# Routing per chunk into fixed regions of rows, and expert outputs added to the output by accumulating DMAs

## The reference

```python
x = x + attention(layernorm(x), Wq, bq, Wk, bk, Wv, bv, Wo, bo)   # 32 heads of 16, 8 key/value heads
xf = layernorm(x).reshape(2048, 512)
gate_logits = xf @ gate_w.T                                        # 8 experts
top_vals, top_idx = top_k(gate_logits, 2)
w = softmax(top_vals)
y = einsum('td,eod->teo', xf, expert_w) + expert_b
out = x + sum over the token's two experts of w * y
```

## Time and profile before

| | us |
|---|---|
| three runs | 1798.77, 1800.97, 1801.69 (median 1800.97) |
| the profiled execution | 1808.37 |
| its span | 1806.6 |
| PE, DVE, ACT, POOL busy | 1662.1, 1411.3, 1258.0, 485.4 |

### The profile page before, as it was taken

The page is one execution under the profiler, slowest core; times in us unless marked ns, Lnnn a source line. Parts: engine busy times, 40 slices in busy tenths (PEclk is TensorE's granted clock), DMA queues, the critical chain, the costliest instruction groups (busy, mean ns, idle before and its releaser), DMA issues.

```text
span 1806.6 us, 38059 instructions
## 1 busy us (share of the span) xinstructions
PE 1662.1 (92%) x13766; PEld 799.8 (44%) x13767; DVE 1411.3 (78%) x1401; ACT 1258.0 (70%) x2349; POOL 485.4 (27%) x730
## 2 busy tenths in 40 slices
PE   5999999999999999999999999999999979569970
PEld 3533444444444444444444444444444446328860
DVE  3287899999999999999999999999999316451214
ACT  2324788888888888888888888888888953313320
POOL 3121033222232233222223222222223351150016
PEclk9997899999999999999999999999999999669995
DMA  6346312321241232223121211121121331144447
GB/s 195 87 117 138 47 43 45 60 73 40 52 86 40 40 60 63 46 52 81 44 54 41 58 30 30 34 52 29 29 52 34 128 105 54 41 174 151 163 136 253
DMA packets 74539, 138.14 MB, mean 76 GB/s; under 512 B 19321, under 2 KB 23433, under 8 KB 73649
## 3 DMA queue, kind: packets, MB, share of 16 engines
q1 hardware_dynamic: 46352, 80.25, 18.4%
q0 software_dynamic: 25616, 54.21, 10.9%
q10 hardware_dynamic: 2448, 1.84, 0.6%
HBM read 82.61 MB, written 52.17 MB: 75 GB/s over the span
## 4 chain that ended last, share of the span: by engine, by line
PE 88%; POOL 3%; issue 2%; DMA 2%; DVE 2%; ACT 1%; ACTq 1%; SPq 0%; POOLq 0%; DVEq 0%
PE bank L815 33%; PE bank L776 24%; PE bank L805 16%; PE bank L896 8%; PE bank L748 3%; POOL slots_x L444 1%; PE bank L958 1%; POOL ys L453 1%; POOL xs L453 1%; DVE max_kc L1068 1%; PE bank L763 1%; DMA x_all<-in_L_attn_x 1%; PE bank L908 1%; DMA q_st<-q_parts 0%; PE bank L738 0%
## 5 line engine op out<-in xcount | busy, mean ns | idle before, releaser
L1068 DVE TENSOR_REDUCE max_kc<-bank 128x1 f32<-128x1024 f32 x1024 | 1241.5, 1222 | 84.7 <-PE bank L776 65.0
L652 ACT ACTIVATE arena_p<-bank 128x512 f32<-128x512 f32 x2048 | 1109.4, 595 | 171.3 <-PE bank L805 141.2
L815 PE MATMUL bank<-arena_p,v_cur 128*32 128x256 f32 x8192 | 660.5, 395 | 5.6 <-issue 5.6
L776 PE MATMUL bank<-k_st,q_st 48*128 48x512 f32 x2048 | 514.2, 500 | 5.3 <-DMA q_st<-q_parts 3.9
L805 PE MATMUL bank<-q_st,k_st 50*128 50x512 f32 x2048 | 449.6, 411 | 0.3 <-ACT arena_p L652 0.3
L776 PEld LDWEIGHTS bank<-k_st,q_st 48*128 48x128 f32 x2048 | 192.2, 185 | 434.4 <-issue 382.4
L805 PEld LDWEIGHTS bank<-q_st,k_st 50*128 50x128 f32 x2048 | 298.5, 187 | 35.4 <-ACT arena_p L652 22.4
L815 PEld LDWEIGHTS bank<-arena_p,v_cur 128*32 128x32 f32 x8192 | 163.1, 108 | 296.2 <-issue 155.0
L379 POOL DMA_DIRECT2D sums<-o_acc x128 | 63.9, 506 | 330.8 <-ACT o_acc L632 328.0
L1185 DVE TENSOR_TENSOR x2T_lo<-bank,x2T_hi 128x512 fp32r<-128x512 f32 x39 | 27.0, 692 | 105.8 <-ACT x2T_hi L662 105.8
L748 PE MATMUL bank<-xT,arena_p 128*128 128x512 f32 x160 | 82.4, 639 | 2.8 <-ACT xT L592 2.8
(11 more groups left out here) (151 smaller groups left out, 913.3 us busy)
## 6 DMA issues: line engine op xcount, KB each, us to landing
q_st<-q_parts SPq DMA_DIRECT2D x192, 128.0 KB, 4.7
slots_x<-be_sb POOLq DMA_DIRECT2D x39, 256.0 KB, 2.4
xs<-slots_x SPq DMA_DIRECT2D x39, 256.0 KB, 2.7
slots_y<-ys SPq DMA_DIRECT2D x39, 256.0 KB, 2.0
q_parts<-parts SPq DMA_DIRECT2D x16, 512.0 KB, 3.0
we_raw<-in_L_ffn_expert_w POOLq DMA_DIRECT2D x8, 1024.0 KB, 6.1
at_parts<-o_hl POOLq DMA_DIRECT2D x128, 64.0 KB, 2.2
k_st<-k_parts SPq DMA_DIRECT2D x48, 128.0 KB, 4.7
```

Source lines behind the costliest of these rows:

```text
L652: act.activation(probs[:, u % PRING, :], bank[:, ring_bank(("score", u)), :], ACT.Exp, scale=SCALE).then_inc(p_ready, 1)
L776: return pe.matmul(bank[:, 2 + 2 * (m % 2) + q, :], q_st[r:r + CROW, j % SLOTS, h, qt * P:(qt + 1) * P], k_st[r:r + CROW, j // NC % KSLOTS ...
L815: mm = pe.matmul(bank[32 * h:32 * h + 32, 6, half], v_cur[:, kt, :], probs[:, (REP * kt + h) % PRING, half], start=(kt == 0 and part == 0) ...
L1068: dve.reduce_max(max_kc[:, m:m + 1], bank[:, 2 + 2 * (m % 2):4 + 2 * (m % 2), :].rearrange("p a s -> p (a s)"), AX.X).then_inc(m_done, 1)
```

## The change

The region of an expert is now fixed: expert e owns the rows from e x 2048 on, so that a chunk's tokens can be placed as soon as that chunk's logits are there. `slots_x` grows from 39 to 135 tiles of rows (8 x 16 and 7 spare ones), and a row from 512 to 516 values: behind the normalised token stand its number, its first expert and the difference of its two logits (twice). All 135 tiles are prefilled with a row whose token number, 4095, lies beyond the output; this takes one DMA of 5 tiles per round, in 27 rounds, and stands between `divide_outputs` and `shift_lo`.

Choosing, ranking and placing run once per chunk of 4 tiles, between tiles of the output projection. After chunk 1, 2048 pairs are placed, and at least S1 = 9 tiles of them are full; these are listed (`full_tiles`) and go through the expert pass first. The other 30 are listed in four parts between the first tiles of the expert pass (`other_tiles`), after the last chunk's rows are known.

The normalised tile is made by ACT in place (`normalise_tile`), after SP has stored the residual tile to the output (`store_residual`). POOL, not DVE, subtracts five of the eight expert matrices. In the expert pass DVE works out each row's gate from the values behind the row (`row_gates`), ACT multiplies by it, DVE adds the gated bias (`row_bias`), and POOL adds the tile to the output rows with an indirect accumulating DMA (`add_rows`), each issued only when the one before has landed. `slots_y`, the biases' matmuls and the gathering are gone.

```diff
@@ POOL
+            def fill_rows(z):
+                n = min(FILL, NX - z)
+                if z > 0:
+                    pool.wait_ge(fill_dma, 16 * (z // FILL))
+                pool.dma_start(slots_x[z * P:(z + n) * P, :].rearrange("(n p) d -> p n d", p=P),
+                               pad_row[:, :].unsqueeze(1).to_broadcast([P, n, W])).then_inc(fill_dma, 16)
...
                 divide_outputs(i)
+                if FILL * (i - 1) < NX:
+                    fill_rows(FILL * (i - 1))
                 if i < N - 1:
                     shift_lo(i + 1)
...
-            for n in range(NKT):
-                pool.wait_ge(xn2_ready, n + 1)
+            def scatter(n):
+                pool.wait_ge(xg_ready, n + 1)
                 for a in range(2):
                     pool.indirect_dma_start(slots_x, bass.IndirectOffsetOnAxis(ap=slot_i[:, a, n:n + 1], axis=0),
-                                            xn2[:, n % SR, :], None).then_inc(sc_dma[n % SR], 16)
+                                            x2_all[:, n, :], None).then_inc(sc_dma[n // TT], 16)
+            def add_rows(s):
+                pool.wait_ge(yb_ready, s + 1)
+                if s > 0:
+                    pool.wait_ge(add_dma, 16 * s)
+                pool.indirect_dma_start(out_rows, bass.IndirectOffsetOnAxis(ap=tok_i[:, s % TRING, :], axis=0),
+                                        ys[:, s % SR, :], None, bounds_check=T - 1, oob_is_err=False,
+                                        compute_op=ALU.add).then_inc(add_dma, 16)
...
+            for e in range(POOL_LO):
+                expert_lo(e)
+            for c in range(NC - 1):
+                pool.wait_ge(slots_ready, c + 1)
+                for t in range(TT):
+                    scatter(c * TT + t)
+            pool.wait_ge(slots_ready, NC)
+            for t in range(TT):
+                add_rows(t)
+                scatter((NC - 1) * TT + t)
+            for s in range(TT, NS):
+                add_rows(s)
@@ SP
+            for c in range(EARLY_C):
+                sp.wait_ge(sc_dma[c], 32 * TT)
+            sp.wait_ge(list_ready, 1)
+            for s in range(SR):
+                load_slots(s)
+            sp.dma_start(x2_all[:, 0:E, 0:D], expert_b.partition_broadcast(P)).then_inc(be_dma, 16)
+            for s in range(SR, S1):
+                load_slots(s)
+            for c in range(EARLY_C, NC):
+                sp.wait_ge(sc_dma[c], 32 * TT)
+            sp.wait_ge(list_ready, 2)
@@ ACT
+            def output_evac(s):
+                n, b = number(s), ring(s)
+                act.wait_ge(y_full, n + 1)
+                act.wait_ge(gate_ready, n + 1)
+                if not first_pass(s):
+                    act.wait_ge(add_dma, n * 16 - 16 * (SR - 1))
+                act.activation(ys[:, b, :], bank[:, b, :], ACT.Identity, scale=gate[:, b, :]).then_inc(y_evac, 1)
@@ PE
             def logits_back(k):
                 pe.wait_ge(lgT_ready, k + 1)
+                if k > 0:
+                    pe.wait_ge(rank_read, k)
@@ DVE
+            for n in range(NKT):
+                residual_add(n)
                 if n == 1:
                     reciprocal_sums(N)
+                statistics(n)
+                scaling(n)
+                if n >= 7 and n % TT == 3:
+                    choose_experts(n // TT - 1)
+                if n >= 9 and n % TT == 1:
+                    place_rows(n // TT - 2)
+                if n == TT * EARLY_C + 6:
+                    full_tiles()
+                if n >= 14:
+                    expert_lo(n - 9)
+            expert_lo(E - 1)
...
+            def row_bias(s):
+                n, b = number(s), ring(s)
+                expert = dve.value_load(expert_i[0:1, bass.ds(n, 1)], min_val=0, max_val=E - 1)
+                dve.wait_ge(y_evac, n + SR + 1)
+                dve.scalar_tensor_tensor(ys[:, b, :], x2_all[:, bass.ds(expert, 1), 0:D].squeeze(1), gate[:, b, :],
+                                         ys[:, b, :], ALU.mult, ALU.add).then_inc(yb_ready, 1)
...
+            place_rows(NC - 2)
+            choose_experts(NC - 1)
+            dve.wait_ge(list_ready, 1)
+            transposed_lo(0)
+            row_gates(0)
+            for s in range(HEAD):
+                slot_step(s)
+                if s == 1:
+                    place_rows(NC - 1)
+                if 2 <= s < 6:
+                    other_tiles(s - 2)
```

More of the change, by code:

```diff
@@ L305, in preln_attention_moe, with number, lap, later @@
         B_MAX = ring_bank(("maxima", 0))
+        HEAD, UNROLL = S1 + 1, TRING
+        LAPS = (NS - HEAD) // UNROLL
+        REST = HEAD + LAPS * UNROLL
+        def number(s):
+            return s if isinstance(s, int) else HEAD + s[0] * UNROLL + s[1]
+        def lap(s):
+            return s // SR if isinstance(s, int) else s[0] * (UNROLL // SR) + (HEAD + s[1]) // SR
+        def later(s, d):
+            return s + d if isinstance(s, int) else (s[0], s[1] + d)
+        def ring(s, size=SR):
+            return (s if isinstance(s, int) else HEAD + s[1]) % size
+        def first_pass(s):
+            return isinstance(s, int) and s < SR
         block = ctx.enter_context(nc.Block())
@@ L571, in _ @@
+            for s in range(SR, S1):
[3 more added lines that the diff above has]
+            sp.wait_ge(list_ready, 2)
+            for s in range(S1, HEAD):
+                load_slots(s)
+            with sp.Fori(0, LAPS) as m:
+                for j in range(UNROLL):
+                    load_slots((m, j))
+            for s in range(REST, NS):
+                load_slots(s)
         @block.scalar
@@ new lines, in slot_step @@
+            def slot_step(s):
+                if s != NS - 1:
+                    transposed_hi(later(s, 1))
+                    difference_exp(later(s, 1))
+                output_evac(s)
+            transposed_hi(0)
+            difference_exp(0)
+            for s in range(HEAD):
+                slot_step(s)
+            with act.Fori(0, LAPS) as m:
+                for j in range(UNROLL):
+                    slot_step((m, j))
+            for s in range(REST, NS):
+                slot_step(s)
@@ L994, in slot_step @@
                         [lambda k: we_hi[:, bass.ds(expert, 1), k, :].squeeze(1),
                          lambda k: we_lo[:, bass.ds(expert, 1), k, :].squeeze(1)]).then_inc(y_full, 1)
+                if s == 1:
+                    ranks(NC - 1)
             pe.wait_ge(elo_ready, E)
-            pe.wait_ge(expert_ready, 1)
-            pe.wait_ge(bias_done, 2 + NKT)
-            transpose_slots(0, 0)
-            with pe.Fori(0, NS // SR) as m:
-                for b in range(SR):
-                    slot_step(m * SR + b, b)
@@ L1004, in _ @@
-            for s in range(NS // SR * SR, NS):
-                slot_step(s, s % SR)
+            pe.wait_ge(list_ready, 1)
+            transpose_slots(0)
+            for s in range(HEAD):
+                slot_step(s)
+            with pe.Fori(0, LAPS) as m:
+                for j in range(UNROLL):
+                    slot_step((m, j))
+            for s in range(REST, NS):
+                slot_step(s)
         @block.vector
@@ new lines, in _ @@
+            place_rows(NC - 2)
[3 more added lines that the diff above has]
+            row_gates(0)
+            for s in range(HEAD):
+                slot_step(s)
+                if s == 1:
+                    place_rows(NC - 1)
+                if 2 <= s < 6:
+                    other_tiles(s - 2)
+                if s == 6:
+                    dve.wait_ge(list_ready, 2)
+            with dve.Fori(0, LAPS) as m:
+                for j in range(UNROLL):
+                    slot_step((m, j))
```

630 lines of the change are left out of this document (309 added, 321 removed).

## The result

| | us |
|---|---|
| after, median of 8 runs | 1813.34 (1807.32 to 1820.47) |
| before, median of 8 runs beside them | 1798.24 (1795.45 to 1801.69) |
| ratio | 1.0092, 95% interval 1.0067 to 1.0117 |
| profiled execution of after, its span | 1809.88, 1808.1 |
| PE, DVE, ACT, POOL busy | 1653.4, 1432.6, 1272.3, 538.6 |

A forecast was written before the change was run, and what follows sets the result against it. PE was taken to bound all but 122 us. Attention adds 0, DVE is free at 1570, adds start at 1582.6, take 168.5, closing 2: span 1753, time 1747 us, range 1702 to 1798.

The forecast's parts named there:

- the price of one add: Expert pass: each accumulating DMA waits for the landing before; a step taken as 4.3 us, the first four 4.5.
- The step of 3.8: Expert pass: by the skill's page alone, 3.04 + 0.78 = 3.8 us per add, time 1727; not used in the sum.
- The bounds of 3.04 and 6.4: Step of an add in us: from below a scatter, 3.04; from above a scatter and full gather in a row, 6.4.
- Rival 3: Expert pass: adds slower than what they replace; break-even at A = 5.7 us, at 6.4 time 1829; chance 0.11.
- a step of 4.9 to 5.7 from any cause: Expert pass: add step in that range in us, grouped with rival 2; time 1770 to 1801, together 0.14.
- The start of the adds: After routing: DVE free at 1570, POOL waits for the last chunk's `place_rows(3)` and starts adding at 1582.6 us.
- POOL is not late: Output projection and routing: POOL's five `expert_lo` (5.1 us each) and 16 scatters (1.3 each) are over near 1550 us.
- The tail: End of kernel: 2 us of closing after the last add's end at 1751.1, giving 1753.
- rival 4: Attention: prefills taking over 15 us meet the shift copies, 2 us in each of 27 rounds; slower, chance 0.03.
- The cold first product: Start of expert pass: after idling, PE's first product costs 5.33 us instead of 2.76, at 1.2 GHz.
- Rival 1: Expert pass: adds hide at a step of 3.6 us or less and PE paces; time 1699 to 1721, chance 0.20.
- Rival 2: Expert pass: DVE's `row_bias` holds POOL's adds, 0.75 us each, step 5.05, time 1776; chance 0.14 shared with other causes.

The follow-up runs named there:

- the second array: Kernel after, with odd tiles added to a second DRAM tensor with its own semaphore, not brought into the output: 1725.1 us.
- the merge: Kernel after with two arrays, the second added to the output at the end by four direct accumulating DMAs: median 1749.6 us, ratio to before 0.9744.

## Why the prediction was wrong

**The step that failed is the price of one add**, "I take 4.3, nearer to the scatter". In the profiled execution the span came to 1808.1 instead of 1753, which splits into three parts: the first add began at 1584.9 instead of 1582.6 (2.3), from there to the last add's start were 211.4 instead of 168.5 - 4.3 = 164.2 (47.2), and the end came 11.8 instead of 6.3 after it (5.5). The rest to the median is that this execution was 3.5 us under its own median, while that of before was 7.4 over the median that the forecast started from.

The step was built from the right pieces with wrong sizes:

| piece of a step, us | forecast | measured | from |
|---|---|---|---|
| from a landing to the next start | 0.30 | 0.83 | after's chain |
| issue | 1.0 | 1.56 | POOL's rows of adds |
| fixed rest until landing | 1.74, bytes of a write in it | 1.14 | 2.70 - 1.56 |
| bytes, 256 KB added | 0.78 more, and 0.4 of a load beside it | 2.13 | 4.83 - 2.70 |
| DVE's hold on POOL | 0.1 | 0.03 on average | below |
| step | 4.3 | 5.7 | |

The 0.30 came from scatters, which wait for nothing between them. Behind a wait for a landing the start takes 0.83 instead, also where the DMA only writes (0.84 in the run with rows written). For the bytes I counted one more transfer at the engines' share. Writing 256 KB costs 0.63 us; adding them costs 2.13, more than three times that. The Trainium skill ("Collectives: The Full Stack", the bandwidth ceiling) says of the rings of collectives that the add costs nothing and only the second read does. The step of 3.8 worked out from it was 1.9 us too short. Of these, 0.53 are the start after a landing, of which the page says nothing; in the rest the measurement doesn't agree with it, since the adding also lengthens the issue by 0.58 us and the bytes by 1.5, where one more transfer was put at 0.78. The bounds of 3.04 and 6.4 held, and nothing in the rows said where between them the step lies; their middle, 4.7, would still have been 1.0 short.

**Rival 3 came true**, with the chance of 0.11, but only in part by its own mechanism: the adds are slower than what they replace. Its point was A = 5.7; measured are 5.56 on average over 38 steps (5.7 for full tiles). By the step alone this is the branch "a step of 4.9 to 5.7 from any cause", forecast faster than before. And a read of the target that comes wholly ahead of the write, A = 6.4, was not seen; no run here can separate the read from the write. What made it slower are the other terms, which moved the point down. With the start and the tail as measured, and attention where the profiled execution of before has it (10.3 us later), the end is 1595.2 + 38 A + 11.8, and equals 1806.6 at A = 5.25. At 5.56 this gives 1818.4, 11.8 us or 0.65% above before; the medians differ by 0.92% (0.67 to 1.17%), and what makes up the rest is open.

**The start of the adds**, forecast at 1582.6, was nearly met only by the luck with the clock. Measured from the last shift copy it should have been 1582.6 - 1422.4 = 160.2 and was 172.8, so this step was wrong by 12.6 us. It says "POOL is not late: its five `expert_lo`" and looks at POOL only; what they do to DVE is not priced. The run without them on POOL has 161.9, so 10.9 of the 12.6 are gone when DVE does the five itself. I had read only half of the contention between the two, a DVE instruction that holds POOL's scatter. Here POOL's subtraction holds DVE's small ones. The Trainium skill ("SBUF — State Buffer", who interferes with whom, and the summary of rules) states it: a DVE instruction with two inputs in SBUF contends with a GpSimd instruction that reads SBUF, and the second one to issue waits until the first is finished. The trace agrees, with 12.38 us for a step of 0.16, and goes beyond it: the step began in the first of three subtractions of 4.5 us and got through only behind the third.

**The tail** was put at 2 us behind the last landing. The kernel before showed the 11.1 us from its last gather to its end, and I did not read it as a term, since DVE and SP work in it.

**What was right.** Attention cost nothing: PE is busy 1260 of 1266 us before, and the table of stages shows the same after; the fills of rival 4 landed in 5.8 us and delayed no round. The cold first product, DVE as the one that sets the start, and the chain of 39 landings as the term that decides all showed up. Rival 1 (PE paces) did not come, but it is what the second array brings: 1701 to 1715 forecast without a merge, 1725 measured.

**Rival 2** (DVE's `row_bias` holds POOL) has a real mechanism and almost no price. Two of the 39 adds, each with the `row_bias` beside it:

```profile
1701.32 1.56 POOL L510 DMA_INDIRECT out_y<-ys,tok_i  x1 [4.15 <-DMA out_y<-ys,tok_i]
1701.35 0.75 DVE L1385 SCALAR_TENSOR_TENSOR ys<-x_all,gate,ys 128x512 f32<-128x512 f32 x1 [3.78 <-ACT ys L806]
...
1706.60 0.75 DVE L1385 SCALAR_TENSOR_TENSOR ys<-x_all,gate,ys 128x512 f32<-128x512 f32 x1 [3.32 <-ACT ys L806]
1706.78 2.00 POOL L510 DMA_INDIRECT out_y<-ys,tok_i  x1 [3.91 <-issue]
```

In 29 of the adds `row_bias` began after the add had started, most often by 0.02 to 0.11 us, and the issue took 1.56 to 1.61 us. In three it was running already, and the issue took 2.00, 1.99 and 1.66 us: 1.0 us in all. So it is the order of the two starts that decides, and here it fell well by a few hundredths of a microsecond. The scatter of 2.30 us is the same case and not a rare accident: it started while DVE's subtraction ran. So did one or two scatters in the kernel after and in each of eight of its edits, all of them of 1.9 to 2.9 us, while those that started up to 0.5 us ahead of such a subtraction kept their 0.97. The rule that the prediction names for it speaks of DVE's two-port mode; no row shows the mode, only that all of these DVE instructions read two tiles in SBUF.

The runs also show how the loss divides. Giving DVE the subtractions takes 11 us off and makes the kernel equal to before within the interval. Letting two adds be under way takes 82 us off the chain, of which the merge takes 24 back. So it is the order "each add after the landing of the one before" that cost more (82 us over PE's pace) than the gathering did (57 us).

## What to carry to other kernels

A chain of DMAs that each wait for the one before is priced by a full round: restart, issue, fixed latency and bytes; here 5.7 us for 256 KB added to DRAM rows, of which only 2.1 go by bytes. Before such a chain replaces parallel work, multiply it by its length, and compare it with the pace of the engine that it must keep up with (here 3.2 us); two targets with a merge at the end can be far cheaper than one. When work is moved to POOL, look at which small DVE instructions read two tiles in SBUF at that time, for they may wait for the whole of it, and for the next ones behind it.

## What was not expected of the hardware

- An accumulating indirect DMA of 128 rows has an issue of 1.56 us on POOL, with or without a bounds check and for rows of 1 or 2 KB; a writing one 0.98, for rows of 1 or 2 KB.
- From issue to landing: added 2.70 us with no real row, 3.8 with 1 KB rows, 4.83 with 2 KB rows; written 2.1 with no real row, mostly 2.35 to 2.62 with 1 KB rows, 2.73 with 2 KB rows.
- Two such adds to different tensors overlap: one started every 3.2 us, PE's pace, and the chain of 39 took 129.5 us instead of 211.4.
- An add that starts while a DVE instruction with two tiles in SBUF is running has an issue of up to 2.0 us instead of 1.56; one that starts 0.02 us ahead of it isn't held.
- Four direct accumulating DMAs from DRAM to DRAM took 22.5 us for 4 MB.
- A DVE instruction on 128 x 1 values took 12.38 us beside three of POOL's subtractions in a row, with 0.16 us alone; one that reads a single tile took 0.16 beside them too.
- The span ends 10.2 to 13.6 us after the start of the last indirect add (6.7 to 10.9 after the landing of POOL's last DMA); a load by SP in that time changes nothing. The cause stays open.
